# GpSimd instead of VectorE normalises x from batch 2 on, in a gated cross-attention and ternary feed-forward kernel

## What is computed

```
xn    = (x - mean(x)) / sqrt(var(x) + eps)            # per row of 512
theta = theta_w @ context + b;  phi = phi_w @ xn + b;  g = xn.T @ g_w
p     = softmax(theta.T @ phi);  t = p @ g            # 512 x 512 scores
h     = relu(norm(t) * gamma + beta)                  # one mean and variance a batch
x     = x + tanh(gate0) * (out_w @ h + b + context)
y     = norm(x);  a = quant8(rmsnorm(y))
f     = silu(a @ w1q.T) * (a @ w2q.T)                 # w1q, w2q, w3q ternary
out   = x + tanh(gate1) * (quant8(rmsnorm(f)) @ w3q.T)
```

## Time and profile before

| | before |
|---|---|
| median of 3 runs (lowest to highest) | 300.6 us (300.51 to 300.93) |
| the profiled execution's own time | 300.9 us |
| its span | 298.9 us |
| TensorE busy | 294.7 us, 99% of the span |
| VectorE busy | 241.2 us, 81% |
| ScalarE busy | 197.2 us, 66% |
| GpSimd busy | 193.8 us, 65% |
| granted TensorE clock | full in every slice |

### The profile page before, as it was taken

One profiled execution on the slowest core, in us unless ns is written; L12 is line 12 of the kernel. 1 busy time (PEld: TensorE's weight loads), 2 busy tenths in 40 slices (PEclk: granted clock), 3 DMA queues, 4 the chain that ended last, 5 costly groups with the idle time before them and its releaser, 6 DMA issues.

```text
span 298.9 us, 4419 instructions
## 1 busy us (share of the span) xinstructions
PE 294.7 (99%) x1350; PEld 160.1 (54%) x1350; DVE 241.2 (81%) x541; ACT 197.2 (66%) x347; POOL 193.8 (65%) x293
## 2 busy tenths in 40 slices
PE   8999999999999999999999999999999999999996
PEld 5765757575757566644444444444444444444444
DVE  3799889796969797899888788887986896876872
ACT  1389898989989877699954736455465547445720
POOL 3351789594949286666988778586786786665610
PEclk9999999999999999999999999999999999999999
DMA  7999970094320002010326366144324342561456
GB/s 252 411 418 414 405 281 3 16 385 163 140 71 0 0 3 35 0 38 0 70 52 77 83 127 114 40 110 106 72 70 106 73 111 64 102 109 50 93 101 183
DMA packets 52936, 37.00 MB, mean 124 GB/s; under 512 B 43056, under 2 KB 43696, under 8 KB 51888
## 3 DMA queue, kind: packets, MB, share of 16 engines
q1 hardware_dynamic: 52624, 36.45, 42.5%
q10 hardware_dynamic: 288, 0.27, 0.3%
HBM read 22.02 MB, written 4.19 MB: 88 GB/s over the span
## 4 chain that ended last, share of the span: by engine, by line
PE 93%; ACT 4%; DMA 2%; SPq 0%; DVE 0%; issue 0%
PE bank L1149 37%; PE bank L1167 17%; PE bank L1093 9%; PE bank L1071 7%; PE bank L1108 5%; PE bank L1086 4%; PE bank L1058 4%; PE bank L1048 4%; PE bank L1037 4%; ACT wq L492 2%; DMA c_sb<-ctx_in_dram 2%; PE bank L1180 1%; ACT prob L539 1%; ACT probT L535 1%; PE bank L1120 0%; PE bank L1116 0%
## 5 line engine op out<-in xcount | busy, mean ns | idle before, releaser
L1149 PE MATMUL bank<-wq,stage 128*128 128x512 bf16 x512 | 113.3, 379 | 0.0
L1149 PEld LDWEIGHTS bank<-wq,stage 128*128 128x128 bf16 x512 | 50.1, 98 | 61.5 <-issue 2.3
L816 DVE SCALAR_TENSOR_TENSOR stage<-bank,s,stage 128x512 f32<-128x512 f32 x64 | 47.5, 744 | 22.2 <-PE bank L1149 18.2
L573 ACT ACTIVATE xn<-stage 128x1024 f32<-128x1024 f32 x31 | 32.8, 1057 | 46.2 <-DVE stage L816 46.2
L565 ACT ACTIVATE stage<-bank,s 128x512 f32<-128x512 f32 x64 | 43.2, 681 | 16.3 <-PE bank L1149 14.3
L1167 PE MATMUL bank<-wq,prob 128*128 128x512 bf16 x224 | 50.5, 379 | 0.0
L428 POOL TENSOR_SCALAR stage<-stage,hsc 128x1024 f32<-128x1024 f32 x30 | 33.4, 1123 | 20.3 <-DVE hsc L847 20.3
L346 POOL TENSOR_SCALAR prob<-prob,rsum 128x512 f32<-128x512 f32 x29 | 19.6, 694 | 30.9 <-DVE rsum L718 30.9
L821 DVE TENSOR_REDUCE m<-stage 128x1 f32<-128x1024 f32 x31 | 37.7, 1216 | 0.8
L1167 PEld LDWEIGHTS bank<-wq,prob 128*128 128x128 bf16 x224 | 21.9, 98 | 26.4
L1071 PE MATMUL bank<-ph,th 128*128 128x512 f32 x96 | 36.0, 487 | 0.0
(11 more groups left out here) (117 smaller groups left out, 434.3 us busy)
## 6 DMA issues: line engine op xcount, KB each, us to landing
stage<-w1t_dram SPq DMA_DIRECT2D x4, 1024.0 KB, 11.5
stage<-w2t_dram SPq DMA_DIRECT2D x4, 1024.0 KB, 14.6
stage<-w3t_dram SPq DMA_DIRECT2D x4, 1024.0 KB, 5.8
x<-x_dram SPq DMA_DIRECT2D x7, 512.0 KB, 10.8
c_sb<-ctx_in_dram SPq DMA_DIRECT2D x7, 512.0 KB, 6.3
out_dram<-stage SPq DMA_DIRECT2D x14, 256.0 KB, 2.3
pc<-pack_c_dram SPq DMA_DIRECT2D x1, 640.0 KB, 15.5
x<-x_dram SPq DMA_DIRECT2D x2, 256.0 KB, 3.4
```

The source lines that it names most:

```text
L573: A.activation(junk, h_sb[t % 2][:, half * HF:(half + 1) * HF], ACT.Square, accum_out=ssq[:, half:half + 1]).then_inc(sq_done, 1)
L816: V.scalar_tensor_tensor(h_sb[k][:, c * 512:(c + 1) * 512], up_banks(n)[1][:, :], s12[:, u % 2, 1, k:k + 1], sil[n % 3], ALU.mult, ALU.mul ...
L1149: last = mm(bank[:, :], turned[:, row:row + P], wq[:, at:at + 512], start=q == 0, stop=q == KI - 1)
```

## The change

From batch 2 on, `x_norm` moves from VectorE to GpSimd, where it stands directly behind `tx_root(i - 2)`, with the same two tensor_scalar instructions for each batch (twelve in all, for batches 2 to 7). In turn 1 there is no tx_root yet, so it stands directly behind x_root(2). Batches 0 and 1 stay on VectorE. Two waits on VectorE change with it: the aggregation of the statistics, which overwrites `xmv`, now waits for `xn_ready` of the batch before instead of for its root, and `residual(b)`, which overwrites x, waits from batch 2 on until x has been normalised.

```diff
+            def x_norm(b):
+                pool.wait_ge(xrstd_ready, b + 2)
+                pool.wait_ge(proj_done, 3 * b)
+                for o in range(DH):
+                    G.tensor_scalar(xn[:, o], x2[:, (2 * b + o) * T:(2 * b + o + 1) * T], xmv[:, o, 0:1], xrs[:, o:o + 1],
+                                    ALU.subtract, ALU.mult).then_inc(xn_ready, 1)
...
                 if i >= 2:
                     tx_root(i - 2)
+                if i + 1 < B:
+                    x_norm(i + 1)
                 if i == 2:
                     rounds(0, 0, 4)
...
                     link.wait(dve)
-                    dve.wait_ge(xrstd_ready, b + 1)
+                    dve.wait_ge(xn_ready, 2 * b)
                     for k in range(DH):
...
             def residual(b):
                 for o in range(DH):
+                    if b >= 2:
+                        dve.wait_ge(xn_ready, 2 * b + 2)
...
                 row_max(i, 2)
-                if 1 <= i < B - 1:
-                    x_norm(i + 1)
                 row_max(i, 3)
```

## The result

| | before | with the change |
|---|---|---|
| median (lowest to highest) | 300.73 us (300.51 to 300.93), 4 runs | 302.59 us (302.51 to 303.14), 4 runs |
| profiled execution, its span | 300.9, 298.9 us | 302.63, 300.6 us |

What follows compares the result with a forecast made beforehand. The prediction took TensorE, busy 99% of the span, to bound the kernel. Its terms, -0 (VectorE's pairs) + 0 (GpSimd's work in idle time) + 0.1 (turn 1), gave +0.1 us: 300.7 us, range 300.2 to 301.2.

Steps and rivals of the forecast that it cites:

- The nearest row is `gated_context`, the same operation ... 0.767 us: Price of GpSimd's new x_norm instruction, taken from another row of the profile: 0.767 us each, 1.53 us a pair.
- GpSimd's 9.2 us in idle time: Sum's term for all six pairs on GpSimd: 9.2 us of work lying in its idle time, costing 0.
- 1.53 fits: Turn 2: the pair fits GpSimd's 1.84 us idle before the weight scale, with 0.3 to spare.
- 2.1 us are left: Turns 3 to 5: rounds move back 1.53 us into 3.65 us idle before `normalise`, leaving 2.1 us.
- So `normalise`, for which turned probabilities on TensorE wait, is not moved.: GpSimd, turns 2 to 6: the idle gaps hold the pairs, so `normalise` starts no later.
- GpSimd as the new bound: Slower rival: a 1.4 us instruction gives 300.7 to 301.0 us; `normalise` moves only above 1.8 us; chance 0.02.
- VectorE's pairs, worth 0: Twelve instructions leaving VectorE, 7.7 us busy, gain 0 at the end; other bound 0.29 us from turn 2.
- The new waits, worth 0: Waits of phi, the statistics and `residual`: phi's costs nothing, the others are met a turn earlier.
- xn early: Turn 3: xn ready near 54.1, 1.9 us earlier than before and 5.3 us before phi(4) needs it.
- Turn 1, +0.1: Second addition of residual(1) waits behind GpSimd, delaying row_max and ScalarE's chain: 0.1 us, bounds 0 and 0.32.
- The alternation: VectorE and GpSimd take turns on SBUF, one instruction each, so an addition stands behind one GpSimd instruction.
- 0.77 us instructions in place of 1.11 us ones make such a hold-up no longer: Other turns: the pair meets `tx_norm` on VectorE as rounds do now, without longer hold-ups; nothing there waits tightly.

Runs made afterwards that it cites:

- experiment 1: Kernel without the reference's computation: single tensor_scalar and tensor_tensor forms on GpSimd alone, then VectorE alone; GpSimd (add, mult) 767 or 768 ns, (subtract, mult) about 2.07 us.
- experiment 2: Changed kernel with x_norm adding a mean negated in x_root: 301.18 us, ratio 1.0009; with that negation from batch 2 on only: 300.73 us, ratio 1.0000.
- experiment 6: Changed kernel with tx_root and x_norm ahead of the first weight rounds in turns 3 to 5 and of prep_root in turn 6: 300.92 us, ratio 1.0003.
- experiment 7: Kernel before, no work added, with tx_root behind all four weight rounds in turns 3 to 5: 302.99 us, ratio 1.0069.
- experiment 4: Changed kernel's new waits on VectorE only, with VectorE normalising every batch as before: 300.83 us, ratio 1.0007.
- experiment 9: Kernel without the reference's computation: rows of five VectorE instructions beside three of GpSimd's; three cheap GpSimd instructions beside additions took 4.68 us, 2.3 alone.

## Why the prediction was wrong, step by step

- **"The nearest row is `gated_context`, the same operation ... 0.767 us": the step that failed.** Same opcode, operands and size, but (add or mult) against (subtract): 2.075 us alone (experiment 1), 2.3 in the kernel. The sum's term "GpSimd's 9.2 us in idle time" was 27.8 us. Experiment 2 shows that this step decided: at the cheap price nothing is lost. It doesn't show that the rest of the working was right; that the absolute times agree (300.73 us measured, 300.7 forecast) is chance in part, since the kernel before measured 300.80 beside it and 300.6 when the forecast was made. With the true price the working would have looked for the loss in the wrong place, as the next three points say.
- **"1.53 fits", "2.1 us are left".** With 4.4 to 4.6 us neither gap holds the pair (1.84 and 3.65 in the earlier trace rows). The overflow of turn 2 does not have "the whole of the gap before 58.85 behind" it: ahead of that gap stand `normalise` at 43.95, with 0.73 us idle before it, and the first rounds and tx_root of turn 3, with none.
- **"So `normalise`, for which turned probabilities on TensorE wait, is not moved."** It moved by 2.0 us in turn 4, and this was the wrong place to look: 1.8 us of such lateness are free (experiment 6). The result with little slack is tx_root's, of which the prediction says only that the pair meets `tx_norm` and that "nothing there waits tightly". Before, in turns 3 to 6, it was ready 0.7 to 1.1 us ahead of its use, so no row of the waits showed it; an order that makes it 3 us late in three turns costs 2.2 us (experiment 7).
- **"GpSimd as the new bound"**, given 0.02, is the rival that came true, past its own threshold of 1.8 us. That threshold was itself wrong: the gaps of 1.84 and 0.73 us hold a pair of 2.57, so `normalise` of turn 3 moves from 1.3 us an instruction on, and by my estimate tx_root of turn 3, ready 0.72 us ahead of its use, is waited for from about 1.6 on. Its mechanism was incomplete too, since it looked at `normalise` only. The low chance rested on the price row alone.
- **VectorE's pairs, worth 0:** right. In experiment 2 VectorE is 6.8 us less busy and the time the same.
- **The new waits, worth 0:** right (experiment 4). **xn early:** at the cheap price it is early by microseconds, as worked out (experiment 2); at the true price hardly. In turns 5, 6 and 7 phi's first weight load names GpSimd's xn, with 0.24 to 0.26 us idle, where the same step took 0.24 before, so nothing is lost; but the pair ends at 74.53, 90.38 and 106.90 us, only 0.05 to 0.2 ahead of that load. A slightly slower pair would have opened a second path for the loss.
- **Turn 1, +0.1:** 0 in size, wrong in kind. The second addition was to stand behind GpSimd; the trace after has GpSimd behind both additions:

```profile
21.64 1.28 DVE L715 TENSOR_TENSOR x<-c_sb,x 128x512 f32<-128x512 f32 x2
21.97 2.82 POOL L335 TENSOR_SCALAR xn<-x,xmv,xrs 128x512 f32<-128x512 f32 x1
```

The additions take the 1.28 us of the earlier trace rows, and `values(1, 0)` is at 35.08, not later. The alternation read from the earlier trace rows was that of two VectorE tensor_scalars with rounds, and does not hold for additions (experiment 9).
- **"0.77 us instructions in place of 1.11 us ones make such a hold-up no longer":** the longer row was not the new pair. The rounds, shifted beside residual(b), took 3.16 instead of 2.23 us, and the additions 2.02 instead of 1.28 (turn 4).

What stays open is how those meetings (in turn 4, 0.9 us on the rounds and 0.7 on the additions) and the 4.6 us of the pair share the loss of turns 4 to 6; no run kept the one without the other there.

## What to carry to other kernels

A price taken from a neighbour's row must match in the operation codes too, on GpSimd above all: if the trace has no row of the very form, measure the form by itself or work out from which price on the forecast turns, with every gap on the way (the prediction said 1.8 us, the gaps give 1.3), and give that case more than a token chance. Where work goes onto an engine whose later results are waited for, look at each result behind it in the queue, the one-column ones first, and ask when it is read; a wait that the profile doesn't list may be met with only 0.7 us to spare. And where the order is yours, put the short instruction that others need ahead of the long ones that nobody needs soon: that alone gave back 1.7 us here.

## What the runs showed of the hardware

- GpSimd's tensor_scalar on 128x512 float32 takes 767 or 768 ns for (add, mult), (mult, add) and (mult, mult) and 2069 to 2075 ns for (subtract, mult), (mult, subtract), (add, add) and (max, mult), all with two per-partition operands; at 128x1024 it is 1193 ns for (add, mult) against 3779 for (subtract, mult) (experiment 1). The Trainium skill (GPSIMD Engine Reference, section 3.1) puts the best case at about 1.8 cycles an element and gives 769 ns for 512 elements: the trace agrees for the first group, and is 2.7 times that for the second.
- In experiment 9 five back-to-back VectorE additions took 3.5 us beside GpSimd's 0.77 us instructions and beside its 2.07 us ones alike, against some 3.05 us free (0.69 and four steps of 0.59, from the pair's 1.28 us). The Trainium skill (SBUF — State Buffer, section Who interferes with whom) has the later one wait for the whole of the other instruction; by the trace the hold-up by a long GpSimd instruction was about 0.5 us, not its 2 us, while GpSimd's first instruction waited for about three additions.
